# The key-length term of the attention heads, made by ScalarE with keys on partitions and turned into the score banks

## Chip, cores and metric

The kernel runs on one core of one Trainium2 chip. The metric is device microseconds from launch to end, the median of several runs. All data here is 32-bit float.

## What is computed

The kernel computes four small transformer layers one after another. The change touches only the attention of the last layer: 8 sequences of 512 tokens, 16 heads of 64 complex elements. Cut to what matters, for one head:

```python
qn = (q.real ** 2 + q.imag ** 2).sum(-1)          # length of each query
kn = (k.real ** 2 + k.imag ** 2).sum(-1)          # length of each key
E = exp(clip(-mu * |i - j|, -30, 0))              # depends on i - j alone
s = einsum('bihd,bjhd->bhij', qr, conj(kr)).real  # turned queries and keys
maha = maximum(qn[i] + E*E * kn[j] - 2 * E * s, 0) / V
logits = coef * log1p(maha / nu) - 0.5 * DH * log(V)
A = softmax(where(i >= j, logits, -inf));  out = A @ v
```

The kernel works with this expression divided by a function of i - j, so that a score is `s` plus a table times `kn[j]` plus another table times `qn[i]`. Every table depends on i - j alone. Before the heads start, each table lies in memory as one row per head, and is loaded so that partition p holds the row shifted by p. The lengths come out of the program with a factor of -0.5.

## The kernel before

The work of the heads is cut into 64 **pairs** m (a pair is two heads of one sequence: 8 sequences times 8 head pairs, 8 consecutive pairs sharing weights and tables) and each pair into two **units** g = 2m + e, one per head. A unit has four blocks i of 128 queries. Only the key blocks j <= i are worked on, ten blocks of 128 x 128, in three pieces p: `PIECES` (L3153) is block 3 (512 keys), blocks 1 and 0 (256 and 128 keys), block 2 (384 keys).

The order of the work is written out by hand. Each engine has a function (`heads_pe` L3173, `heads_dve` L3291, `heads_act` L3384, `heads_pool` L3492) with a loop `for m in range(-4, PAIRS + 1)` that issues its steps in one fixed order, for several pairs at once (a software pipeline). One pass through it is called a **turn** below. Each engine works through its list strictly in order and waits on counting semaphores (`k.after`). The SP queue issues the DMAs (`heads_loads` L2688).

A unit passes through these steps:

- TensorE `project` (L3176): queries (x = 0) and keys (x = 1) of a pair, two matrix products of 512 columns each, into banks 2 and 3. VectorE `products` (L3294) multiplies them by cosines and sines, GpSimd `rotate` (L3504, instructions L3511 and L3512) adds them, and the SP queue's `move` (L2677) copies the result by DMA to `qk`, of which there are two, for even and odd pairs.
- ScalarE `square` (L3387) squares `qk`. TensorE `norms` (L3188) sums over the elements into bank 1, ScalarE `lengths` (L3396) copies, TensorE `sums` (L3198) turns, and ScalarE `norms` (L3403) writes `nn`: the lengths with tokens on partitions. The squares of the keys are written in reverse order, so `nn` holds key lengths in reverse.
- GpSimd `norms` (L3495, instruction L3501) multiplies `backwards`, a matrix with ones on its anti-diagonal, by the key lengths: `dk`, four blocks of 128 x 128 for a unit.
- TensorE `scores` (L3206), one piece: for each query block a product of queries and keys into bank 4 + e, and for each of its key blocks a product of a table block with a block of `dk`, accumulated onto it.
- VectorE `query_norms` (L3309) adds the query term and moves the piece to `y`; `distance` (L3326); ScalarE `logarithm` (L3412); VectorE `logits` (L3337, a custom instruction with a minimum at L3346); ScalarE `exponential` (L3420).
- TensorE `flip` (L3226) turns each block, ScalarE `turned` (L3432) copies it to `pt`, TensorE `values` (L3252) multiplies by the values, which `project_values` (L3241) and ScalarE `values` (L3443) made. VectorE `reciprocals`, ScalarE `outputs` (L3451) and GpSimd `accumulate` (L3514, instruction L3524) close a unit.

Bank 4 + e holds one piece at a time: `scores` waits until `query_norms` has emptied it of the piece before. Products (`mm`, L74) show in the profile as line L75, transpositions (`tr`, L77) as L79. Both helpers issue one call, but the profile shows two MATMUL instructions with their weight loads for each 32-bit product and one for each transposition:

```python
def mm(self, out, lhsT, rhs, start=True, stop=True):
    return self.T.matmul(out, lhsT, rhs, start=start, stop=stop, skip_group_check=True)

def tr(self, out, in_, start=True):
    n = in_.shape[0]
    return self.T.matmul(out, in_, self.ident[0:n, 0:n], start=start, stop=True,
                         is_transpose=True, skip_group_check=True)
```

## Time and profile before

| | us |
|---|---|
| runs | 3070.5, 3072.42, 3085.04 |
| median | 3072.42 |
| the profiled execution | 3083.46, of which the span is 3082.2 |
| busy in the span: TensorE / VectorE / ScalarE / GpSimd | 2946.1 / 2434.7 / 1807.0 / 884.1 |
| mean granted clock of TensorE | 0.972 |

The span runs from the first to the last instruction of the profiled execution. Busy time is the time in which an engine has an instruction under way. Instructions of one engine overlap a little, so that the time to the next start is shorter than the duration shown. The heads start at about 1611 us and run to the end of the span; the rest is the earlier layers, which the change leaves alone.

### The profile page before, as it was taken

The numbers are of one execution on the slowest core, as the hardware profiler recorded it, in microseconds if no ns is written. First come the engines' busy times: TensorE is split into PE (matmuls) and PEld (weight loads), VectorE is DVE, ScalarE is ACT, GpSimd is POOL, SyncE is SP. The second block draws the span as 40 slices with busy tenths as digits, with TensorE's granted clock in tenths as the row PEclk, the third lists the DMA queues.
The fourth block names the chain that finished last, engine by engine and source line by source line (L and its number), as shares of the span: only waits on it lengthen the run. The fifth ranks groups of instructions, "written<-read, shape, count | busy, mean of one in ns | idle before, by whom it ended". The sixth has DMA issues, their size and how long they took to land. (4 is left out here: it accounts for less than half of the span.)

```text
span 3082.2 us, 55344 instructions
## 1 busy us (share of the span) xinstructions
PE 2946.1 (96%) x19062; PEld 2235.2 (73%) x19062; DVE 2434.7 (79%) x4760; ACT 1807.0 (59%) x4118; POOL 884.1 (29%) x839
## 2 busy tenths in 40 slices
PE   6999998999999999999687999999999999999998
PEld 4777775566666677787575787877878777878777
DVE  5878876566557555456766999999999999999997
ACT  3455544655645444434464777677777676776776
POOL 2111101101101100000433444444444444444442
PEclk8999999999999899999898999999999999999999
DMA  2000001000000000000402223232232323223221
GB/s 57 2 5 15 28 15 52 1 1 1 1 1 1 1 1 1 1 1 1 115 1 55 49 59 76 58 73 49 57 76 59 76 59 76 58 50 76 47 49 44
DMA packets 79513, 111.66 MB, mean 36 GB/s; under 512 B 15942, under 2 KB 32521, under 8 KB 79241
## 3 DMA queue, kind: packets, MB, share of 16 engines
q1 hardware_dynamic: 75266, 105.77, 14.3%
q8 instruction: 158, 2.59, 0.4%
q10 hardware_dynamic: 3974, 2.37, 0.3%
q14 instruction: 115, 0.93, 0.1%
HBM read 34.43 MB, written 6.55 MB: 13 GB/s over the span
## 5 line engine op out<-in xcount | busy, mean ns | idle before, releaser
L3346 DVE CUSTOM_DVE_ANT_0 scratch<-scratch,tb,coef 128x512 f32<-128x512 f32 (+3 forms) x512 | 552.9, 1115 | 1.3 <-ACT scratch L3418 1.3
L75 PE MATMUL banks<-lower 128*128 128x128 f32 (+2 forms) x2688 | 510.6, 356 | 1.4 <-DMA lower<-in_L_w2T 0.8
L75 PEld LDWEIGHTS banks<-lower 128*128 128x128 f32 (+1 forms) x2688 | 346.3, 195 | 166.4 <-issue 165.2
L75 PEld LDWEIGHTS banks<-scratch,tb 128*128 128x128 f32 x2560 | 357.3, 192 | 101.9 <-issue 61.9
L75 PE MATMUL banks<-scratch 128*128 128x256 f32 (+3 forms) x1088 | 378.1, 433 | 11.4 <-ACT scratch L3026 8.9
L3511 POOL TENSOR_TENSOR normed<-normed,aT 128x512 f32<-128x512 f32 x128 | 176.7, 1381 | 709.4 <-DVE aT L3304 426.0
L75 PE MATMUL banks<-scratch,tb 128*128 128x128 f32 x2560 | 369.4, 275 | 0.0
L75 PEld LDWEIGHTS banks<-n,pt 128*128 128x128 f32 x2560 | 300.8, 192 | 54.8 <-ACT pt L3440 51.1
L75 PE MATMUL banks<-n,pt 128*128 128x128 f32 x2560 | 323.5, 278 | 3.1 <-ACT moe L3459 3.1
L83 DVE SCALAR_TENSOR_TENSOR scratch<-scratch,tb 128x512 f32<-128x512 f32 (+3 forms) x512 | 320.8, 656 | 2.3
L83 DVE SCALAR_TENSOR_TENSOR scratch<-tb,nn,banks 128x512 f32<-128x512 f32 (+3 forms) x512 | 263.7, 535 | 41.1 <-PE banks L75 41.1
L3418 ACT ACTIVATE scratch<-scratch 128x384 f32<-128x384 f32 (+1 forms) x384 | 213.3, 556 | 137.6 <-DVE scratch L83 137.6
L3428 ACT ACTIVATE scratch<-scratch,mn 128x512 f32<-128x512 f32 (+3 forms) x512 | 288.0, 568 | 3.9 <-DVE mn L3346 3.9
L75 PE MATMUL banks<-nT,w 128*128 128x512 f32 x544 | 265.5, 610 | 10.5 <-DVE normed L3307 6.5
L1481 DVE TENSOR_TENSOR lower<-lower,banks 128x512 f32<-128x512 f32 x160 | 108.9, 685 | 157.7 <-ACT lower L1694 157.7
L3440 ACT ACTIVATE pt<-banks 128x384 f32<-128x384 f32 (+1 forms) x384 | 199.7, 528 | 48.9 <-PE banks L79 48.8
L79 PE MATMUL banks<-ident,scratch 128*128 128x128 f32 x1408 | 219.3, 273 | 3.0 <-ACT scratch L3428 2.1
L1694 ACT ACTIVATE lower<-banks 128x512 f32<-128x512 f32 x160 | 94.2, 597 | 199.2 <-PE banks L75 199.1
L75 PEld LDWEIGHTS banks<-scratch 128*128 128x128 f32 x1088 | 172.2, 192 | 47.1 <-issue 33.2
L3501 POOL TENSOR_TENSOR scratch<-backwards,nn 128x512 f32<-128x512 f32 x128 | 164.3, 1304 | 64.4 <-ACT nn L3410 64.4
L3459 ACT ACTIVATE moe<-banks,rs 128x128 f32<-128x128 f32 x512 | 145.6, 371 | 54.9 <-PE banks L75 54.9
L79 PEld LDWEIGHTS banks<-ident,scratch 128*128 128x128 f32 x1408 | 167.6, 142 | 8.3 <-issue 3.7
(433 smaller groups left out, 5448.3 us busy)
## 6 DMA issues: line engine op xcount, KB each, us to landing
scratch<-normed SPq DMA_DIRECT2D x512, 128.0 KB, 2.4
tb<-head_rows SPq DMA_DIRECT2D x32, 512.0 KB, 8.5
turn<-head_turns SPq DMA_DIRECT2D x32, 128.0 KB, 3.5
xs<-in_x SPq DMA_DIRECT2D x8, 256.0 KB
head_turns<-loads SPq DMA_DIRECT2D x8, 256.0 KB, 2.5
head_turns<-rotation SPq DMA_DIRECT2D x8, 256.0 KB, 2.8
w<-in_L_Wqk SPq DMA_DIRECT2D x8, 256.0 KB, 3.2
out<-xs SPq DMA_DIRECT2D x8, 256.0 KB, 2.3
```

Of the source, the lines that this page charges most:

```text
L75: return self.T.matmul(out, lhsT, rhs, start=start, stop=stop, skip_group_check=True)
L79: return self.T.matmul(out, in_, self.ident[0:n, 0:n], start=start, stop=True, is_transpose=True, skip_group_check=True)
L83: return self.V.scalar_tensor_tensor(out, a, s, b, op0, op1)
L1481: V.tensor_tensor(k.hidden[:, e % 2, m, b * S:(b + 1) * S], k.gated_h[:, m, :], k.bank(2 * m + 1), ALU.mult).then_inc(*k.l1_hid[m].up())
L1694: A.activation(k.gated_h[:, m, :], k.bank(2 * m), ACT.Silu).then_inc(*k.l1_silu[m].up())
L3346: x = V.tensor_tensor_reduce(y, y, view(hd["tb"][:, e, 2, i * P + 127:i * P + 128], [[-1, n]]), k.coef[:, h:h + 1], 3e38, ALU.add, ALU.min ...
L3418: A.activation(y, y, ACT.Ln, bias=1.0).then_inc(*k.h_ln.up())
L3428: x = A.activation(y, y, ACT.Exp, bias=t["mn"][:, i:i + 1], scale=-1.0, accum_out=t["sum"][:, i:i + 1])
L3440: A.activation(t["pt"][:, lo:hi], k.bank(6 + f % 2)[:, 0:hi - lo], ACT.Identity).then_inc(*k.h_pt.up())
L3459: x = A.activation(t["o"][:, i, :], k.bank(0)[:, i * P:(i + 1) * P], ACT.Identity, scale=t["rs"][:, i:i + 1])
L3501: G.tensor_tensor(t["dk"][:, :, :], k.backwards[:, :].unsqueeze(1).broadcast_to([P, 4, P]), r["nn"][:, :, 2 + e].unsqueeze(2).broadcast_to ...
L3511: G.tensor_tensor(re, re, k.sines[:, 1, :], ALU.subtract)
```

## The change

The key term of a unit is now made by ScalarE (`key_norms`): for each key block j, one activation reads the table of the key term with key p of the block on partition p and the queries from block j on along the row, and scales every partition by the length of its key. That gives `gk`, four tiles of 512, 384, 256 and 128 columns, of which there is one set per head e (before, `dk` had four). `scores` now first turns these blocks into the score bank with transpositions, and then accumulates the products of queries and keys onto them. The step of GpSimd goes away, and so do `backwards` and the reverse order of the squares. The table is loaded with another offset, by six DMAs of the same total size rather than four. The order of the steps in all four loops is new. Where the table's semaphore is waited for, 96 stands in place of 64.

```diff
@@ -2632,9 +2632,12 @@
         k.lengths = k.w1s.rearrange("p g h -> p (g h)")
         k.pairs3 = [dict(qk=flat[:, 2048 * j:2048 * j + 2048].rearrange("p (x e s) -> p x e s", x=2, e=2),
                          nn=k.sb(f"nn3_{j}", [P, TPB, 4])) for j in range(2)]
+        w2 = k.w2s.rearrange("p g d -> p (g d)")
+        gk = [[flat[:, a:b] for a, b in ((9216, 9728), (9728, 10112), (10112, 10368), (10368, 10496))],
+              [flat[:, 10496:11008], w2[:, 0:384], flat[:, 11008:11264], w2[:, 384:512]]]
         pt3 = [k.sb(f"pt3_{j}", [P, 1280]) for j in range(2)]
         k.lanes3 = [dict(y=flat[:, 4096 + 1280 * j:5376 + 1280 * j],
-                         dk=flat[:, 9216 + 512 * j:9728 + 512 * j].rearrange("p (t c) -> p t c", c=P),
+                         gk=gk[j % 2],
                          pt=pt3[j % 2], v=k.n[:, TPB * (j % 2):TPB * (j % 2) + TPB, :],
                          o=k.moe[:, TPB * (j % 2):TPB * (j % 2) + TPB, :],
                          mn=k.sb(f"mn3_{j}", [P, 4]), sum=k.sb(f"sum3_{j}", [P, 4]),
...
@@ -2670,9 +2673,9 @@
     def load_tables(self, hp):
         k, j = self, hp % 2
         for e in range(2):
-            for first in (0, 2):
-                k.Y.dma_start(k.head[j]["tb"][:, e, first:first + 2, :],
-                              k.spread(2 * hp + e, first, 2, 384)).then_inc(*k.h_tb[j].up(16))
+            for first, n, at in ((0, 2, 384), (2, 1, 384), (3, 1, 0)):
+                k.Y.dma_start(k.head[j]["tb"][:, e, first:first + n, :],
+                              k.spread(2 * hp + e, first, n, at)).then_inc(*k.h_tb[j].up(16))
 
     def move(self, m, x):
         k, Y = self, self.Y
...
@@ -3113,8 +3116,6 @@
-                k.fill(k.backwards[:, :], 0.0)
-                k.keep_where(k.backwards[:, :], ALU.not_equal, 1.0, 1 - P, [[1, P]], 1)
...
@@ -3210,17 +3211,18 @@
             k.after(T, k.h_mv, 128 * (m + 1))
             k.after(T, k.h_dk, g + 1)
             if m % SEQS == 0:
-                T.wait_ge(k.h_tb[m // SEQS % 2].sem, 64 * (m // SEQS // 2 + 1))
+                T.wait_ge(k.h_tb[m // SEQS % 2].sem, 96 * (m // SEQS // 2 + 1))
             k.after(T, k.h_qn, k.pieces(m, p, e) - 2)
-            at = 0
+            rows, at = [], 0
             for i in k.PIECES[p]:
-                n = (i + 1) * P
-                ps = k.bank(4 + e)[:, at:at + n]
-                k.mm(ps, r["qk"][:, 0, e, i * P:(i + 1) * P], r["qk"][:, 1, e, 0:n], stop=False)
+                rows.append((i, k.bank(4 + e)[:, at:at + (i + 1) * P]))
+                at += (i + 1) * P
+            for i, ps in rows:
                 for j in range(i + 1):
-                    x = k.mm(ps[:, j * P:(j + 1) * P], hd["tb"][:, e, 3, (i - j) * P:(i - j + 1) * P],
-                             t["dk"][:, 3 - j, :], start=False)
-                at += n
+                    k.tr(ps[:, j * P:(j + 1) * P], t["gk"][j][:, (i - j) * P:(i - j + 1) * P],
+                         start=(i == rows[0][0] and j == 0))
+            for i, ps in rows:
+                x = k.mm(ps, r["qk"][:, 0, e, i * P:(i + 1) * P], r["qk"][:, 1, e, 0:(i + 1) * P], start=False)
             x.then_inc(*k.h_sc.up())
 
         def flip(g, p):
...
@@ -3264,29 +3266,29 @@
 
         for m in range(-4, k.PAIRS + 1):
             values(2 * m - 1, 2)
-            flip(2 * m, 2)
+            scores(2 * m + 2, 2)
             scores(2 * m + 3, 2)
             sums(m + 2)
+            flip(2 * m, 2)
             project(m + 3, 1)
             project_values(2 * m + 1)
             flip(2 * m + 1, 0)
+            values(2 * m, 0)
+            flip(2 * m + 1, 1)
+            values(2 * m, 1)
+            flip(2 * m + 1, 2)
             scores(2 * m + 4, 0)
             scores(2 * m + 5, 0)
-            flip(2 * m + 1, 1)
-            values(2 * m, 0)
-            values(2 * m, 1)
+            scores(2 * m + 4, 1)
             values(2 * m, 2)
-            flip(2 * m + 1, 2)
             project(m + 4, 0)
-            scores(2 * m + 4, 1)
+            project_values(2 * m + 2)
             flip(2 * m + 2, 0)
             scores(2 * m + 5, 1)
-            project_values(2 * m + 2)
-            scores(2 * m + 4, 2)
             values(2 * m + 1, 0)
+            values(2 * m + 1, 1)
             flip(2 * m + 2, 1)
             norms(m + 3)
-            values(2 * m + 1, 1)
 
     def heads_dve(self):
         k, V = self, self.V
...
@@ -3313,7 +3315,7 @@
-                V.wait_ge(k.h_tb[m // SEQS % 2].sem, 64 * (m // SEQS // 2 + 1))
+                V.wait_ge(k.h_tb[m // SEQS % 2].sem, 96 * (m // SEQS // 2 + 1))
...
@@ -3356,30 +3358,30 @@
             V.reciprocal(t["rs"][:, :], t["sum"][:, :]).then_inc(*k.h_rs.up())
 
         for m in range(-4, k.PAIRS + 1):
-            query_norms(2 * m + 3, 1)
-            products(m + 3, 0, 1)
+            logits(2 * m + 1, 2)
             distance(2 * m + 3, 1)
-            reciprocals(2 * m)
             query_norms(2 * m + 2, 2)
-            distance(2 * m + 2, 2)
-            query_norms(2 * m + 3, 2)
             logits(2 * m + 2, 0)
             logits(2 * m + 3, 0)
+            query_norms(2 * m + 3, 2)
+            distance(2 * m + 2, 2)
             products(m + 3, 1, 1)
-            query_norms(2 * m + 4, 0)
             distance(2 * m + 3, 2)
             products(m + 3, 1, 0)
             logits(2 * m + 2, 1)
-            query_norms(2 * m + 5, 0)
+            query_norms(2 * m + 4, 0)
             logits(2 * m + 3, 1)
             logits(2 * m + 2, 2)
-            reciprocals(2 * m + 1)
+            query_norms(2 * m + 5, 0)
             distance(2 * m + 4, 0)
+            reciprocals(2 * m)
             query_norms(2 * m + 4, 1)
             distance(2 * m + 5, 0)
+            products(m + 4, 0, 0)
+            products(m + 4, 0, 1)
+            query_norms(2 * m + 5, 1)
+            reciprocals(2 * m + 1)
             distance(2 * m + 4, 1)
-            logits(2 * m + 3, 2)
-            products(m + 4, 0, 0)
 
     def heads_act(self):
         k, A = self, self.A
...
@@ -3390,8 +3392,7 @@
-            out = view(k.squares[1][:, 0, S - 1:S], [[S, 2], [-1, S]]) if x else k.squares[0]
-            A.activation(out, r["qk"][:, x, :, :], ACT.Square).then_inc(*(k.h_sk if x else k.h_sq).up())
+            A.activation(k.squares[x], r["qk"][:, x, :, :], ACT.Square).then_inc(*(k.h_sk if x else k.h_sq).up())
...
@@ -3408,6 +3409,20 @@
             k.after(A, k.h_dk, 2 * (m - 1))
             k.after(A, k.h_qn, 6 * (m - 1))
             A.activation(r["nn"][:, :, :], k.bank(1).rearrange("p (i c w) -> p i c w", i=TPB, c=4)[:, :, :, 0], ACT.Identity).then_inc(*k.h_nn.up())
+
+        def key_norms(g):
+            if not 0 <= g < k.UNITS:
+                return
+            m, e, t, r, hd = k.unit(g)
+            k.after(A, k.h_nn, m + 1)
+            if m:
+                k.after(A, k.h_sc, k.pieces(m - 1, 2, e))
+            if m % SEQS == 0:
+                A.wait_ge(k.h_tb[m // SEQS % 2].sem, 96 * (m // SEQS // 2 + 1))
+            for j in range(TPB):
+                x = A.activation(t["gk"][j], view(hd["tb"][:, e, 3, S - 1:S], [[-1, (TPB - j) * P]]),
+                                 ACT.Identity, scale=r["nn"][:, j, 2 + e:3 + e])
+            x.then_inc(*k.h_dk.up())
 
         def logarithm(g, p):
             if not 0 <= g < k.UNITS:
...
@@ -3462,44 +3477,37 @@
 
         k.nc.scalar.preload_act_table_set("natural_log_exp_and_others")
         for m in range(-4, k.PAIRS + 1):
+            exponential(2 * m + 1, 1)
+            logarithm(2 * m + 3, 0)
+            turned(2 * m, 0)
+            lengths(m + 2)
+            exponential(2 * m, 2)
+            logarithm(2 * m + 2, 1)
+            outputs(2 * m - 1)
+            norms(m + 2)
+            turned(2 * m, 1)
+            turned(2 * m, 2)
             exponential(2 * m + 1, 2)
+            key_norms(2 * m + 4)
+            turned(2 * m + 1, 0)
             logarithm(2 * m + 3, 1)
-            norms(m + 2)
             logarithm(2 * m + 2, 2)
-            turned(2 * m, 2)
+            key_norms(2 * m + 5)
+            exponential(2 * m + 2, 0)
+            turned(2 * m + 1, 1)
             values(2 * m + 1)
-            outputs(2 * m - 1)
-            exponential(2 * m + 2, 0)
-            turned(2 * m + 1, 0)
             exponential(2 * m + 3, 0)
-            turned(2 * m + 1, 1)
             square(m + 3, 0)
-            outputs(2 * m)
             logarithm(2 * m + 3, 2)
             turned(2 * m + 1, 2)
             exponential(2 * m + 2, 1)
             logarithm(2 * m + 4, 0)
-            exponential(2 * m + 3, 1)
+            outputs(2 * m)
             values(2 * m + 2)
             square(m + 3, 1)
-            logarithm(2 * m + 5, 0)
-            turned(2 * m + 2, 0)
-            turned(2 * m + 2, 1)
-            exponential(2 * m + 2, 2)
-            logarithm(2 * m + 4, 1)
-            lengths(m + 3)
 
     def heads_pool(self):
         k, G = self, self.G
-
-        def norms(g):
-            if not 0 <= g < k.UNITS:
-                return
-            m, e, t, r, hd = k.unit(g)
-            k.after(G, k.h_nn, m + 1)
-            k.after(G, k.h_sc, 6 * (m - 1))
-            G.tensor_tensor(t["dk"][:, :, :], k.backwards[:, :].unsqueeze(1).broadcast_to([P, 4, P]),
-                            r["nn"][:, :, 2 + e].unsqueeze(2).broadcast_to([P, 4, P]), ALU.mult).then_inc(*k.h_dk.up())
 
         def rotate(m, x):
             if not 0 <= m < k.PAIRS:
...
@@ -3525,12 +3533,10 @@
             x.then_inc(*k.h_acc.up())
 
         for m in range(-4, k.PAIRS + 1):
+            accumulate(2 * m - 2)
             rotate(m + 3, 0)
-            norms(2 * m + 4)
-            norms(2 * m + 5)
             rotate(m + 3, 1)
             accumulate(2 * m - 1)
-            accumulate(2 * m)
 
     def heads_close(self):
         k, V = self, self.V
```

## Rows read from the trace of the kernel before

**Rows 1.** Busy time by stretch: the stage before, the fill, a steady stretch.
```profile
...
core 0: us, PE busy (x) PEld busy (x) DVE busy (x) ACT busy (x) POOL busy (x), PEclk, DMA share, GB/s
1560.00:1600.00 40.00, 36.00 (x232) 30.42 (x232) 28.77 (x59) 32.36 (x73) 13.20 (x17) 1.00 0.00 1
1611.00:1640.00 29.00, 16.74 (x31) 6.10 (x32) 8.16 (x7) 4.32 (x6) 9.51 (x8) 0.65 0.24 55
...
2000.00:2300.00 300.00, 300.00 (x2054) 239.62 (x2053) 295.07 (x515) 212.28 (x569) 140.78 (x108) 1.00 0.28 65
...
```

**Rows 2.** The chain of waits, 2000 to 2100 us: start, us, what.
```profile
...
2002.49 4.43 PE banks L75 x34
...
2024.77 4.43 PE banks L75 x34
...
```

**Rows 3.** TensorE in order of time, part of one turn: start, us, what.
```profile
...
2016.49 1.02 PE L75 MATMUL banks<-scratch 128*128 128x512 f32 x2
2017.35 1.05 PE L75 MATMUL banks<-scratch,tb 128*128 128x128 f32 x8
2018.24 0.49 PE L79 MATMUL banks<-ident,scratch 128*128 128x128 f32 x3
2018.57 2.40 PE L75 MATMUL banks<-n,pt 128*128 128x128 f32 x20
...
2021.13 1.88 PE L75 MATMUL banks<-nT,w 128*128 128x512 f32 x4
2022.85 0.60 PE L75 MATMUL banks<-scratch 128*128 128x256 f32 x2
...
```

**Rows 4.** Groups by shape, 2000 to 2600 us: busy us, mean ns, idle before.
```profile
...
L75 PE MATMUL banks<-scratch,tb 128*128 128x128 f32 x1080 | 155.6, 275 | 0.0
...
L79 PE MATMUL banks<-ident,scratch 128*128 128x128 f32 x537 | 85.0, 273 | 0.0
...
L3459 ACT ACTIVATE moe<-banks,rs 128x128 f32<-128x128 f32 x212 | 60.3, 371 | 20.8 <-PE banks L75 20.8
...
L3418 ACT ACTIVATE scratch<-scratch 128x384 f32<-128x384 f32 x108 | 56.4, 522 | 10.7 <-DVE scratch L83 10.7
...
L3440 ACT ACTIVATE pt<-banks 128x384 f32<-128x384 f32 x108 | 53.2, 492 | 20.3 <-PE banks L79 20.3
L3428 ACT ACTIVATION_READ_ACCUMULATOR scratch<-scratch,mn 128x1 f32 x216 | 44.6, 207 | 0.0
...
L3418 ACT ACTIVATE scratch<-scratch 128x512 f32<-128x512 f32 x54 | 33.7, 624 | 50.6 <-DVE scratch L83 50.6
L3428 ACT ACTIVATE scratch<-scratch,mn 128x384 f32<-128x384 f32 x54 | 32.8, 607 | 0.0
...
```

**Rows 5.** ScalarE in order of time, two neighbours.
```profile
...
2005.29 1.05 ACT L3394 ACTIVATE hT<-scratch 128x1024 f32<-128x1024 f32 x1
2006.24 0.62 ACT L3418 ACTIVATE scratch<-scratch 128x512 f32<-128x512 f32 x1
...
```

**Rows 6.** GpSimd in order of time: key blocks, and both accumulations.
```profile
...
2012.16 2.50 POOL L3501 TENSOR_TENSOR scratch<-backwards,nn 128x512 f32<-128x512 f32 x2 [0.80 <-ACT nn L3410]
...
2021.82 2.73 POOL L3524 TENSOR_TENSOR acc<-acc,moe 128x512 f32<-128x512 f32 x2
...
```

**Rows 7.** VectorE in order of time, the same turn.
```profile
...
2005.08 0.61 DVE L3346 CUSTOM_DVE_ANT_0 scratch<-scratch,tb,coef 128x384 f32<-128x384 f32 x1
...
2010.24 0.58 DVE L83 SCALAR_TENSOR_TENSOR scratch<-tb,nn,banks 128x384 f32<-128x384 f32 x1
...
2012.23 1.52 DVE L3346 CUSTOM_DVE_ANT_0 scratch<-scratch,tb,coef 128x512 f32<-128x512 f32 x1
...
2015.13 1.21 DVE L3304 TENSOR_TENSOR aT<-banks,turn 128x1024 f32<-128x1024 f32 x1
...
```

**Rows 8.** The move's line on the DMA queue: ns min/median/max.
```profile
...
L2685 SPq DMA_DIRECT2D scratch<-normed x512: 461/597/2203, 1618.3 to 3026.3; - x171
...
```

**Rows 9.** The transpositions' line (L79) alone, by stretch.
```profile
...
1560.00:1600.00 40.00, 9.13 (x72) 8.39 (x73) 1.00 0.00 1
...
```

More of the change, by code:

```diff
@@ L2570, in layer3_prepare @@
         k.nT3, k.acc = k.sb("nT3", [D, SEQS, S]), k.sb("acc", [P, SEQS, TPB, D])
-        k.wvo, k.backwards = k.sb("wvo", [D, H, D]), k.sb("backwards", [P, P])
+        k.wvo = k.sb("wvo", [D, H, D])
         k.own, k.mu_scratch = k.sb("own", [P, 2, P]), k.sb("mu_scratch", [P, 2, 256])
```

## The prediction

> **What bounds the kernel now.** I read the busy time by stretch first. In a steady stretch of the heads TensorE is busy for all of 300 us at a granted clock of 1.00, VectorE for 295.07, ScalarE for 212.28, GpSimd for 140.78 [rows 1]. The chain of waits says what ends last: there TensorE's lines alone, the same piece returning after 22.28 us (2002.49, then 2024.77) [rows 2]. So a turn is 22.28 us and TensorE sets it: whatever leaves TensorE shortens the turn until another engine takes over. In the same units a turn has 21.91 us of VectorE (295.07 / 300 x 22.28), 15.77 of ScalarE and 10.46 of GpSimd. VectorE stands only 0.37 us below the bound, so its own gain decides how much of TensorE's can be had.
>
> **What leaves TensorE.** Ten key products a unit, 20 a turn, show as 40 MATMUL instructions a turn (1080 in 27 turns) [rows 4]. Eight follow each other in 0.89 us, from 2017.35 to the next start at 2018.24 [rows 3]: 0.111 each, 4.44 a turn. What comes in are 20 transpositions. They show as one instruction each (537 in 27 turns for the 20 flips), and the mean durations are alike, 275 and 273 ns [rows 4], so the spacing counts: three take 0.33 us (2018.24 to 2018.57) [rows 3], 0.110 each, 2.20 a turn. The products of queries and keys stay. **TensorE: 22.28 - 4.44 + 2.20 = 20.04 us a turn.** I take no price for changing between the two kinds, as three transpositions between products already come out at 0.33; that they now accumulate with products in one bank is not in the trace, and I bound it by 0 and 0.3 us a turn (twelve changes between the two kinds, a quarter of one instruction each).
>
> **What leaves VectorE.** No VectorE instruction goes; its saving is that GpSimd is not beside it. The two steps that go are 2.50 us of GpSimd from 2012.16 [rows 6], and VectorE's two instructions of 512 columns beside them take from 2012.23 to 2015.13, 2.90 us [rows 7] (two such, only the first is shown). One of 384 columns without GpSimd beside it takes 0.61, of which 0.54 until the next start. With 0.15 for 128 more columns that is 0.69, twice 1.38, so the pair lost 1.52 us. Instructions that read a bank lose nothing: 0.58 for 384 columns beside GpSimd at 2010.24 [rows 7]. With that pair gone and all else alike, **VectorE is 21.91 - 1.52 = 20.39 us a turn.** Six GpSimd instructions are left, 10.46 - 2.50 = 7.96 us. At the same price each (0.76) they cost 4.6 of the 20.39, so VectorE's own work is some 15.8. How much comes back depends on what the new order puts beside them. One accumulation now falls, after `outputs(2m)`, on the end of VectorE's list, where `products(m + 4, 0, ...)` read banks: up to 0.8 less. The other five fall on `distance` and `logits` as before. So 19.6 to 20.4.
>
> The Trainium skill, SBUF — State Buffer, "two separate sides", says that such a pair of ports is an exclusive lock and the loser fully blocks. By that, the two customs would have taken 2.50 + 1.38 = 3.88 us where the trace has 2.90, and taking GpSimd away would free 2.50, not 1.52: VectorE 19.4, TensorE alone the bound at 20.04. I go by the trace.
>
> **What ScalarE gets.** Eight activations a turn, per unit 512, 384, 256 and 128 columns. None is in the trace. The nearest are the logarithm (0.62 for 512 columns, 0.52 for 384) and `outputs` with the same kind of scale per partition (0.37 for 128) [rows 4]; for 256 between them, 0.45. Neighbours overlap by 0.10 (1.05 long, next start after 0.95) [rows 5]. That gives 0.52 + 0.42 + 0.35 + 0.27 = 1.56 a unit, 3.12 a turn, **ScalarE 15.77 + 3.12 = 18.9 us.** Bounds: 0.2 less a unit, and up to the price of the exponential instead (0.61 for 384), 0.1 more an activation, 19.7. Below 20.04 in every case, but with 1 us to spare, not 6.5.
>
> **Whether the waits close.** The key term was made by an engine with idle time; now it is queued on ScalarE, behind other steps and ahead of others. After `sums(m + 2)` TensorE has, until it needs `key_norms(2m + 5)` for `scores(2m + 5, 0)`: four flips of together 1.43, a projection of 1.72 (2021.13 to 2022.85), 0.89 for `project_values`, 0.89 and 0.67 for values, 1.30 for the piece of the other unit [rows 3]: 6.9 us. ScalarE has in that time `norms` 0.1, `turned` 0.38 twice, `exponential` 0.60 with the reading of its sum [rows 4], `key_norms` 1.56, `turned` 0.48, two logarithms of 0.41, `key_norms` 1.56: 5.9, and some 0.4 of waiting for `flip(2m + 1, 0)` between them, 6.3. It closes with 0.6 us. The other tight place is bank 4: `scores(2m + 4, 1)` comes right after `scores(2m + 5, 0)`, 1.30 us after the piece that `query_norms(2m + 4, 0)` must empty in 0.67; if VectorE is then inside an instruction that GpSimd holds up, TensorE waits a few tenths. I take **0.16 us a turn** for such places, 20.2, between 0 and what VectorE's unchanged losses give (20.4, and 0.2 more where it waits for TensorE).
>
> **Small ones.** The table's two extra DMA issues fall once in eight turns on the SP queue, at 0.6 us each as its move issues take [rows 8]; hidden by the queue's waits. The key lengths' order in the square costs nothing. The fill, where TensorE stands still more than a third of the time and the clock is at 0.65 [rows 1], gains nothing: 62 turns of 64 count.
>
> **The sum.** 62 x (22.28 - 20.2) = 129 us. The profiled execution took 3083.46, so it would be 2954. That execution lies 11 us above the median of 3072.42; nothing in the change touches where such executions differ, so I set the median at 3072.42 - 129 = **2943 us**.
>
> **Rivals.**
> - *VectorE takes over.* For it: 295.07 of 300 already. It decides if the new order gives back nothing: 20.4 plus waits of 0.3, 20.7, gives 98 us, 2974; if each of the 7.96 us held VectorE up in full, 15.8 + 8.0 = 23.8, past the old bound. Against that end: instructions on banks pass freely. Around 2974: 0.22.
> - *The key term arrives late (the slower end).* In place of the wait for GpSimd, `scores` waits for ScalarE's second `key_norms`. The slack is 0.6 us a turn, and each us beyond it costs 62 us. To lose against before, ScalarE must be 0.6 + 2.24 = 2.9 us later than worked out, which needs activations of about 0.75 rather than 0.39, or a `turned` or `exponential` ahead of them that itself waits for what TensorE does later, a loop. At 4 us late: 20.04 + 3.4 = 23.4, 3145. Against it: no activation of that size in the trace is so slow, and everything ahead in the list has its input from the turn before. 0.07, and 0.03 that it just eats the gain (within 0.5% of no change).
> - *The clock falls.* Transpositions double to 44 a turn, 2.2 per us. In the stage before there were 72 in 40 us, 1.8 per us [rows 9], with the clock at 1.00 and TensorE busy for 36 of 40 [rows 1]; in the fill, with TensorE idle, it went to 0.65. If it fell to the 1.2 GHz level for a tenth of the time, 20.04 / 0.95 = 21.1, 3000. 0.03. The Trainium skill, TensorE: Matmul & The Clock Gate, Part 4, says that transpositions do not count as activity for the gate; by that rule the doubled share speaks against this change, while the stretch just named, a fifth of it transpositions, kept the full clock.
> - *The change does more than I think:* TensorE alone binds, 20.04, 139 us, 2933. It is the lower part of my forecast, not a case apart.
>
> **How the numbers follow.** Forecast (20.04 to 20.4, 2933 to 2955) 0.65, VectorE 0.22, clock 0.03, slower 0.07, no change 0.03. About 0.5% (15 us) is what a measurement of this kernel can tell from no change. Faster by more: 0.90; I give 0.88, as part of VectorE's case reaches up to the old bound. Same 0.04, slower 0.08. The range: below, TensorE's 2933 less 10 for the differences between runs shown, 2923; above, VectorE's case to a turn of 21.1 (73 us), 3000.
>
> **What would show it.** Right: a turn has the 40 MATMUL of the key products no more, and 20 more under the transpositions' line; a turn of 20.0 to 20.4 in the chain, still TensorE's lines; VectorE at 20 us a turn or less and without the two stretched customs; ScalarE near 0.93. Wrong: a turn over 20.7; TensorE's weight loads of `gk` waiting on ScalarE's activation, or of `qk` on VectorE's `query_norms`; a granted clock under 1.00 after 1700 us; the stretched VectorE instructions costing more than 0.76 per GpSimd instruction.

## The result, and the profile after

The changed kernel takes 2947.01 us, the median of four runs (2941.78 to 2952.66), against 3075.39 us before; the ratio is 0.958, with a 95% interval of 0.955 to 0.961. The profiled execution took 2948.47 us. Forecast were 2943 and, for a profiled execution like the one before, 2954.

A **turn** is measured below from one start of TensorE's `norms` to the next. Before, 63 turns took 1399.97 us, nearly all of them 22.28. After, they take 1271.09 us: 128.9 us less. The profiled executions differ by 135.0. The other 6 us lie ahead of the first turn, which starts at 1631.80 before and 1625.14 after. In the profiles of this study that point falls anywhere from 1618.16 to 1637.46, so I count none of it as the change's. The tail behind the last turn is 50.4 us before and 50.6 after.

Busy time by stretch of the changed kernel, a row like that of [rows 1]:

```profile
...
core 0: us, PE busy (x) PEld busy (x) DVE busy (x) ACT busy (x) POOL busy (x), PEclk, DMA share, GB/s
2000.00:2300.00 300.00, 298.19 (x1963) 225.70 (x1961) 289.83 (x566) 282.17 (x745) 119.28 (x89) 1.00 0.31 73
...
```

TensorE is still the bound, but no longer for every nanosecond (298.19 of 300). VectorE is busy for nearly as large a share as before (289.83 against 295.07), in a shorter turn. ScalarE went from 212.28 to 282.17. The granted clock is 1.00.

The chain of waits of the changed kernel, to be held against [rows 2]: start, us, what.

```profile
...
by line: PE banks L75 69.3%; PE banks L79 21.6%; DMA scratch<-normed 3.6%; issue 2.2%; SPq L2688 1.7%; DVE scratch L3348 0.7%; DVE scratch L83 0.7%; DVE normed L3309 0.3%; DVE mn L3348 0.1%; SPq L3162 0.0%; DVEq L3162 0.0%
...
2003.56 2.22 PE banks L75 x18
...
2010.01 0.47 SPq L2688
...
2011.80 3.64 DMA scratch<-normed
2015.52 0.33 DVE normed L3309
...
2024.46 2.22 PE banks L75 x18
...
2044.51 2.22 PE banks L75 x18
...
```

From 2024.46 to 2044.51 is 20.05 us, and so are 22 of the 29 turns that lie between 2000 and 2600 us. From 2003.56 to 2024.46 is 20.90. In that turn the chain leaves TensorE: it goes over the SP queue and the queries' move to VectorE's product, which waits for the move to land.

The groups by shape of 2000 to 2600 us, with [rows 4] for before: of the 20 transpositions of key blocks in a turn 16 stand in the first group, with the 20 flips, and four in the group with the name w2s; the groups of L3423 are `key_norms`.

```profile
...
L79 PE MATMUL banks<-ident,scratch 128*128 128x128 f32 x1061 | 174.8, 274 | 4.8 <-DVE scratch L83 4.7
...
L3423 ACT ACTIVATE scratch<-tb,nn 128x512 f32<-128x512 f32 x59 | 42.3, 717 | 0.0
...
L79 PE MATMUL banks<-ident,w2s 128*128 128x128 f32 x118 | 30.6, 273 | 0.0
L3423 ACT ACTIVATE scratch<-tb,nn 128x256 f32<-128x256 f32 x58 | 29.0, 500 | 0.0
...
L3423 ACT ACTIVATE w2s<-tb,nn 128x384 f32<-128x384 f32 x29 | 17.5, 603 | 0.0
...
L3423 ACT ACTIVATE w2s<-tb,nn 128x128 f32<-128x128 f32 x29 | 11.3, 388 | 0.0
...
```

TensorE in order of time in the changed kernel, around the pieces of block 3 ([rows 3] before), and ScalarE's second `key_norms` of the same turn with the instruction behind it:

```profile
...
2036.35 0.93 PE L79 MATMUL banks<-ident,scratch 128*128 128x128 f32 x7
2037.12 1.02 PE L75 MATMUL banks<-scratch 128*128 128x512 f32 x2
2037.99 0.30 PE L79 MATMUL banks<-ident,scratch 128*128 128x128 f32 x1
2038.13 0.27 PE L79 MATMUL banks<-ident,w2s 128*128 128x128 f32 x1
...
2038.35 0.27 PE L79 MATMUL banks<-ident,w2s 128*128 128x128 f32 x1
2038.46 1.02 PE L75 MATMUL banks<-scratch 128*128 128x512 f32 x2
...
```

```profile
...
2035.98 0.71 ACT L3423 ACTIVATE scratch<-tb,nn 128x512 f32<-128x512 f32 x1
2036.60 0.60 ACT L3423 ACTIVATE w2s<-tb,nn 128x384 f32<-128x384 f32 x1
2037.11 0.49 ACT L3423 ACTIVATE scratch<-tb,nn 128x256 f32<-128x256 f32 x1
2037.51 0.39 ACT L3423 ACTIVATE w2s<-tb,nn 128x128 f32<-128x128 f32 x1
2037.80 0.71 ACT L3443 ACTIVATE scratch<-scratch,mn 128x512 f32<-128x512 f32 x1
...
```

Seven transpositions follow each other in 0.77 us (2036.35 to 2037.12), three flips and four key blocks: 0.110 each, with no price for changing between transpositions and products. Then comes the wait that mattered. The last activation of `key_norms` ends when the next starts to overlap it, about 2037.90, and the transpositions that need it start at 2037.99. The first stands 0.14 ahead of the second rather than 0.11. There is no slack at this place.

### The profile page after: what moved, and what is told of

It reads as the page before. It is cut to its first block and busy times, and to the rows that moved or that the text cites. A ratio compares the mean times of both kernels' runs of the same rounds, so it can differ in the third digit from the quotient of the medians.

```text
span 2946.8 us, 53185 instructions
## 1 busy us (share of the span) xinstructions
PE 2798.7 (95%) x17782; PEld 2064.2 (70%) x17782; DVE 2297.9 (78%) x4760; ACT 2018.7 (69%) x4630; POOL 725.8 (25%) x709
## 5 line engine op out<-in xcount | busy, mean ns | idle before, releaser
L79 PE MATMUL banks<-ident,scratch 128*128 128x128 f32 x2432 | 397.1, 274 | 17.2 <-DVE scratch L83 11.1
L3348 DVE CUSTOM_DVE_ANT_0 scratch<-scratch,tb,coef 128x512 f32<-128x512 f32 (+3 forms) x512 | 396.8, 810 | 0.8 <-ACT scratch L3433 0.8
L79 PEld LDWEIGHTS banks<-ident,scratch 128*128 128x128 f32 x2432 | 294.6, 142 | 114.8 <-issue 95.8
L75 PE MATMUL banks<-scratch 128*128 128x256 f32 (+3 forms) x1088 | 357.3, 433 | 8.9 <-ACT scratch L3029 8.9
L75 PE MATMUL banks<-n,pt 128*128 128x128 f32 x2560 | 344.5, 278 | 4.3 <-ACT moe L3474 4.2
L83 DVE SCALAR_TENSOR_TENSOR scratch<-scratch,tb 128x512 f32<-128x512 f32 (+3 forms) x512 | 343.8, 691 | 0.0
L3519 POOL TENSOR_TENSOR normed<-normed,aT 128x512 f32<-128x512 f32 x128 | 174.2, 1361 | 563.6 <-DVE normed L3309 481.6
L3532 POOL TENSOR_TENSOR acc<-acc,moe 128x512 f32<-128x512 f32 x120 | 164.9, 1374 | 236.3 <-ACT moe L3474 236.3
L3423 ACT ACTIVATE scratch<-tb,nn 128x512 f32<-128x512 f32 (+3 forms) x384 | 199.5, 574 | 0.1
L3309 DVE TENSOR_TENSOR normed<-banks,turn 128x1024 f32<-128x1024 f32 x128 | 156.1, 1220 | 46.0 <-DMA scratch<-normed 37.3
L3520 POOL TENSOR_TENSOR normed<-normed,aT 128x512 f32<-128x512 f32 x128 | 177.9, 1390 | 0.0
```

Of the source, the lines that this page charges most:

```text
L83: return self.V.scalar_tensor_tensor(out, a, s, b, op0, op1)
L3309: V.tensor_tensor(k.turned, k.bank(2, 2), cos_sin, ALU.mult).then_inc(*k.h_cos.up())
L3348: x = V.tensor_tensor_reduce(y, y, view(hd["tb"][:, e, 2, i * P + 127:i * P + 128], [[-1, n]]), k.coef[:, h:h + 1], 3e38, ALU.add, ALU.min ...
L3423: x = A.activation(t["gk"][j], view(hd["tb"][:, e, 3, S - 1:S], [[-1, (TPB - j) * P]]), ACT.Identity, scale=r["nn"][:, j, 2 + e:3 + e])
L3519: G.tensor_tensor(re, re, k.sines[:, 1, :], ALU.subtract)
L3520: G.tensor_tensor(im, im, k.sines[:, 0, :], ALU.add).then_inc(*k.h_rot.up())
```

## The experiments

The turns of all kernels in one table. "Commonest" is the length that occurs most often among the 48 turns from the tenth on (25 and 29 times in the two kernels without key transpositions, 27 times with the idle GpSimd pair, 36 times or more in the others), "mean" the mean over these turns, and the time is the median of the runs, or the only run. Kernels ran on different chips at different times, where the kernel before had medians from 3075 to 3081 us, so the turns compare better than the times.

| kernel | commonest | mean | time |
|---|---|---|---|
| before | 22.28 | 22.28 | 3075 |
| changed | 20.05 | 20.25 | 2947 |
| old term, new order | 22.28 | 22.29 | 3077 |
| new term, old order | 20.80 | 20.89 | 2988 |
| idle GpSimd pair | 20.52 | 20.77 | 2978 |
| no key transpositions | 19.43 | 19.87 | 2931 |
| tables spread | 20.05 | 20.12 | 2955 |
| tables spread, values later | 20.43 | 20.45 | 2965 |
| ScalarE idle step ahead | 20.46 | 20.54 | 2964 |
| ScalarE idle step behind | 20.05 | 20.21 | 2944 |
| key_norms early, values later | 19.98 | 20.04 | 2940 |
| key_norms early | 20.01 | 20.09 | 2948 |
| no key transpositions, key_norms early | 19.43 | 19.87 | 2926 |
| table slivers | 20.05 | 20.14 | 2947 |

**The order without the term.** The kernel before, with the four lists of the changed one; `key_norms` left out, GpSimd's `norms` kept behind `rotate(m + 3, 0)`:

```diff
             accumulate(2 * m - 2)
             rotate(m + 3, 0)
+            norms(2 * m + 4)
+            norms(2 * m + 5)
             rotate(m + 3, 1)
             accumulate(2 * m - 1)
```

> The kernel before with the changed kernel's order on all four engines (key term still by GpSimd and 32-bit products). My theory (the gain is TensorE's 2.24 us a turn, the order only makes room for it): TensorE keeps 22.28 us a turn, VectorE about 19.6 + 1.5 = 21.1, so the turn stays at 22.3 and the time within 10 us of before. Rival (the order is where the gain comes from): turn under 21.5, time under 3025 us. A third way, that the new order doesn't suit the old term: turn over 22.6.

Measured: ratio to before 0.999 (0.9975 to 1.0006), 22.28 us a turn. The order alone gains nothing in time; TensorE's 22.28 holds it. But VectorE says something that nobody expected. Busy time by stretch:

```profile
...
2000.00:2300.00 300.00, 300.00 (x2052) 239.19 (x2051) 266.85 (x513) 208.43 (x565) 138.91 (x108) 1.00 0.28 65
...
```

VectorE is busy for 266.85 us, where it was 295.07 [rows 1]: 19.8 us a turn rather than 21.9, with all eight GpSimd instructions in place. Its list holds the same instructions; they stand beside other company. GpSimd's key pair, and VectorE's instructions around it, in this kernel:

```profile
...
2013.97 2.37 POOL L3501 TENSOR_TENSOR scratch<-backwards,nn 128x512 f32<-128x512 f32 x2 [3.54 <-ACT nn L3410]
...
```

```profile
...
2012.48 0.75 DVE L3346 CUSTOM_DVE_ANT_0 scratch<-scratch,tb,coef 128x512 f32<-128x512 f32 x1
...
2013.16 0.75 DVE L3346 CUSTOM_DVE_ANT_0 scratch<-scratch,tb,coef 128x512 f32<-128x512 f32 x1
...
2013.83 0.61 DVE L83 SCALAR_TENSOR_TENSOR scratch<-tb,nn,banks 128x384 f32<-128x384 f32 x1
2014.36 1.07 DVE L83 SCALAR_TENSOR_TENSOR scratch<-scratch,tb 128x384 f32<-128x384 f32 x1
2015.75 1.23 DVE L3304 TENSOR_TENSOR aT<-banks,turn 128x1024 f32<-128x1024 f32 x1 [0.33 <-PE banks L75]
...
```

The custom instructions of 512 columns, which took 1.52 beside GpSimd [rows 7], take 0.75 here, since they are through before the pair starts. The pair now falls on `query_norms` and on `products`, which read banks, and on one `distance` (1.07 rather than 0.55).

**The term without the order.** The changed kernel with the lists of before:

```diff
             norms(m + 2)
+            key_norms(2 * m + 4)
             logarithm(2 * m + 2, 2)
             turned(2 * m, 2)
+            key_norms(2 * m + 5)
```

> The changed kernel with the orders of before on all four engines, the two key_norms put behind norms(m + 2) and behind turned(2m, 2). If the order hardly matters, TensorE's 20.04 to 20.3 us a turn stays and the time is within 10 us of 2947. My theory: the old order was laid out for a ScalarE with 6.5 us to spare a turn, and now waits appear; turn 20.8 to 21.6, time 2985 to 3035, about half of the gain. If the key term on ScalarE needs the new order altogether: turn 22 or more, 3060 or more.

Measured: 0.970 (0.968 to 0.972), 20.80 us a turn: seven tenths of the gain, more than the half I expected. VectorE is at 292.40 of 300, which is 20.4 us a turn, the 20.39 of the prediction. The rows of its waits, 2000 to 2600 us (total us, times, longest):

```profile
...
PEld banks L79 <- DMA scratch<-normed: 41.3, 34, 1.3
...
PE banks L79 <- DMA scratch<-normed: 15.5, 29, 0.5
DVE scratch L83 <- PE banks L75: 12.2, 29, 0.4
...
```

TensorE now waits in every turn for a move to land, ahead of the first transpositions of a piece, and stands idle for some 0.6 us a turn (it is busy for 291.33 of 300). That is the wait which the old order left no room for.

**GpSimd's company put back.** The changed kernel with two GpSimd instructions of 128 x 512 a turn that write a free buffer:

```diff
             rotate(m + 3, 0)
+            idle(2 * m + 4)
+            idle(2 * m + 5)
             rotate(m + 3, 1)
```

> The changed kernel with two GpSimd instructions of 128 x 512 a turn added where the key blocks used to be made; they write a buffer that nothing reads. If GpSimd's company was a price of its own (1.52 us of VectorE a turn in the kernel before): VectorE 20.5 to 21.2 us a turn rather than 19.6 and the turn 20.5 to 21.3, 15 to 65 us more. Rival (TensorE alone is the bound, VectorE has room): turn unchanged at 20.05 in most turns, mean 20.25, time within 6 us of the changed kernel.

Measured: 20.52 us in most turns, mean 20.77, 2978 us, 31 more. VectorE goes to 297.31 of 300, 20.6 us a turn, 1.1 more. TensorE alone is not the bound: with VectorE beyond 20.5, VectorE's list sets the turn.

**What stands behind TensorE.** No key transpositions; the key-length term is left out:

```diff
-            for i, ps in rows:
-                for j in range(i + 1):
-                    k.tr(ps[:, j * P:(j + 1) * P], t["gk"][j][:, (i - j) * P:(i - j + 1) * P],
-                         start=(i == rows[0][0] and j == 0))
             for i, ps in rows:
-                x = k.mm(ps, r["qk"][:, 0, e, i * P:(i + 1) * P], r["qk"][:, 1, e, 0:(i + 1) * P], start=False)
+                x = k.mm(ps, r["qk"][:, 0, e, i * P:(i + 1) * P], r["qk"][:, 1, e, 0:(i + 1) * P], start=(i == rows[0][0]))
```

> The changed kernel without the 20 key transpositions a turn: the key-length term is left out of the scores, ScalarE still makes its blocks. It asks what binds once TensorE has 2.20 us less, 17.85 a turn. My theory: VectorE with 19.6 and ScalarE with 19.1 us a turn stand right behind, so the turn goes only to 19.3 to 19.8, 28 to 55 us less. Rival (TensorE is the bound and nothing else is near): turn 17.9, 140 us less. Slow turns once in eight, which wait for a move, stay in either case.

Measured: 19.43 us in the commonest turn, mean 19.87, 2930.64 us, though TensorE's own work is 17.85. The commonest turn is in the range that I expected, the time is not: 16 us less rather than 28 to 55, since the turns behind the table loads are now much longer (23.0 to 23.2 in the worst of them). The next bound is 0.6 us below the present one, and an edit of this kind would be worth 0.4 us a turn on the mean, not 2.2. The bound is VectorE's own list: in turns of 19.43 it is never idle (19.43 us busy from 2002.04 to 2021.47), and nearly all its waiting between 2000 and 2600 us is for one thing, the landing of the queries' move (total us, times, longest):

```profile
...
DVE normed L3305 <- DMA scratch<-normed: 13.7, 17, 2.7
...
```

**Whether the second key_norms has slack.** One activation of 384 columns, put ahead of `key_norms(2m + 5)` in one kernel and behind `values(2m + 1)`, after both `key_norms`, in another:

```diff
             logarithm(2 * m + 2, 2)
+            idle(2 * m + 5)
             key_norms(2 * m + 5)
             exponential(2 * m + 2, 0)
             turned(2 * m + 1, 1)
             values(2 * m + 1)
+            idle(2 * m + 5)      (the other kernel)
```

> The changed kernel with one activation of 384 columns (about 0.4 us) added on ScalarE right ahead of key_norms(2m + 5). The prediction had 0.6 us between that step's end and scores(2m + 5, 0); the trace after shows the step ending at 2037.90 and the transpositions starting at 2037.99, next to nothing. If the chain from sums over both key_norms is tight: the turn grows by 0.3 to 0.4, to 20.4, 18 to 25 us more. Rival (ScalarE is busy for 19.06 of 20.05, so 0.4 fits in): turn 20.05 still, within 6 us.

> The same activation, behind values(2m + 1), that is after both key_norms. If only the chain up to key_norms(2m + 5) is tight: the turn stays at 20.05 to 20.1. If ScalarE's list as a whole is tight, wherever the work is put: 20.3 to 20.5, as with the activation ahead.

ScalarE in order of time, with the step ahead:

```profile
...
2036.96 0.51 ACT L3431 ACTIVATE mu_scratch<-nT 128x384 f32<-128x384 f32 x1
2037.37 0.72 ACT L3423 ACTIVATE scratch<-tb,nn 128x512 f32<-128x512 f32 x1
...
```

Measured: the step takes 0.41 us until the next start, and ahead of `key_norms` the turn grows from 20.05 to 20.46, by 0.41, all of it. Behind, it costs nothing: 20.05. ScalarE as a whole has room; the chain through `sums`, `norms` and both `key_norms` to `scores(2m + 5, 0)` has none. It was tight to within hundredths, as the rows of the changed kernel said.

**The long turns.** One or two turns in eight are longer in the changed kernel. The turns are counted from 0 below. First the table loads, one a turn instead of six in one turn:

```diff
...
-            if m % SEQS == 4 and 2 <= hp < k.HEADS // 2:
+            if m % SEQS >= 2 and 2 <= hp < k.HEADS // 2:
                 Y.wait_ge(k.h_sc.sem, 6 * done)
                 Y.wait_ge(k.h_lg.sem, 6 * done)
-                k.load_tables(hp)
+                k.load_tables(hp, m % SEQS - 2)
```

> The changed kernel with its six table loads of every eight turns issued one a turn, behind the keys' move, rather than all six in one turn. Its turns are 20.05 us but for two or three in eight of 20.4 to 21.6, mean 20.25. If the loads in flight hold up the queries' move of the next turn: the longer turn behind the load goes (index 12, 20, 28 ...), the mean falls to 20.12 to 20.18, 4 to 8 us less. If it is a single slow issue on the SP queue that has nothing to do with the loads (there is one of 1.85 us ahead of the load at 2011.80): the turns of index 11, 19, 27 ... stay at 20.9 and less than 4 us come back.

Measured: mean 20.12. The turns behind the loads (index 12, 28, 36, 44, 52) are 20.05 now, those of index 11, 19, 27 and so on stay at 20.3 to 21.0: about two thirds of the excess goes. (This run's 2955 us doesn't show it, since its first turn starts at 1637.46; its 63 turns take 1265.57 us, 5.5 less.) Then, in the changed kernel with its loads in one turn, the transfers cut from 128 partitions to one, so that the later heads' scores are made with wrong tables:

```diff
...
+                q = P if hp < 2 else 1
-                k.Y.dma_start(k.head[j]["tb"][:, e, first:first + n, :],
-                              k.spread(2 * hp + e, first, n, at)).then_inc(*k.h_tb[j].up(16))
+                k.Y.dma_start(k.head[j]["tb"][0:q, e, first:first + n, :],
+                              k.spread(2 * hp + e, first, n, at, q)).then_inc(*k.h_tb[j].up(16))
```

> The changed kernel with its table reloads cut from 128 partitions to one, so that later heads use the first tables (their scores are computed with wrong tables); number and place of the DMA issues are the same, the bytes are gone. If the transfers hold up the moves: all turns 20.05 but for the one slow issue in eight turns, mean 20.12 as with spread loads. If the slow single issue (1.85 us at 2011.80) also comes of the table loads: it goes too, mean 20.05. If the issues alone cost, not the bytes: mean 20.25 stays.

Measured: mean 20.14, the same picture. So the bytes in flight lengthen the turn behind them, and the other long turns (index 11, 19, 27 and so on) don't come of the table loads. In most of these an issue of the queries' move is slow. One in the changed kernel, and one in the kernel with slivers (0.60 is the common length):

```profile
...
2011.80 1.85 SPq L2688 DMA_DIRECT2D scratch<-normed  x1
...
```

```profile
...
2174.22 1.86 SPq L2689 DMA_DIRECT2D scratch<-normed  x1
...
```

But the slow issue alone doesn't explain them. In turns 11, 19 and 35 of the kernel with slivers no issue of this move takes over 0.60 us, and the last still lands 3.25 to 3.65 us after its start rather than the usual 2.4; the turns take 20.49 to 20.89. From the chain of waits in turn 11:

```profile
...
1851.94 0.60 SPq L2689
...
1852.58 3.26 DMA scratch<-normed
...
```

What these turns have in common is a packet on another DMA queue. The queues of the changed kernel from 2009.9 to 2016.5 us, around the slow issue at 2011.80 (packets, MB, share of 16 engines):

```profile
...
q1 hardware_dynamic: 320, 0.52, 34.8%
q8 instruction: 1, 0.02, 1.3%
...
```

The packet on q8, of a kind that the profile calls `instruction`, has 16 KB and lasts from 2011.85 to 2013.27. From turn 4 on, such a packet starts 5 to 7 us behind a turn's start, while the queries' move is under way, in turns 11, 19, 27, 35, 43, 51 and 59 and in no other, in the changed kernel and in the one with slivers alike. These are the long turns that are left (from turn 10 on, but for one of 20.26 with the spread loads). Of the changed kernel's move issues from turn 4 on, 24 of the 25 over 0.9 us overlap such a packet, and 41 of the 439 others. Between two packets lie on average 255.6 to 256.9 TensorE instructions (with those of its sequencer) in each of the fourteen profiles, whether 17.4 or 20.5 us pass between them, so they look like TensorE's own instructions being loaded. All this is read from the traces; no run moved these packets, and the cause is not shown by experiment. The kernel before has slow issues under such packets as well, 2.00 us at 1812.78 for one; nothing waited there.

**Values later.** Spread loads, and the moves started 0.67 us earlier:

```diff
-            values(2 * m - 1, 2)
             scores(2 * m + 2, 2)
             scores(2 * m + 3, 2)
+            values(2 * m - 1, 2)
             sums(m + 2)
```

> As the one before, and on TensorE values(2m - 1, 2) behind the two scores pieces, so that the queries' move starts 0.67 us earlier in a turn and a slow issue has that much more cover. My theory (TensorE binds at 20.05 and only late moves lengthen a turn): mean turn 20.05 to 20.12, 8 to 12 us less than the changed kernel, 2935 to 2939 against 2947. Rival (outputs(2m - 1) comes later by as much and ScalarE's chain is tight): every turn grows by up to 0.5 us, 2950 or more.

Measured: 20.43 us in nearly every turn, mean 20.45, ratio to before 0.963 (0.962 to 0.965). The rival was right. The long turns are nearly gone (20.5 to 20.7), but ScalarE's `outputs(2m - 1)` comes later, and with it `norms` and both `key_norms`. The chain of waits shows where:

```profile
...
2302.84 0.86 PE banks L75 x2
2303.70 0.28 issue
2303.98 0.63 PE banks L79 x4
...
```

TensorE stands still for 0.28 us ahead of the four transpositions of `scores(2m + 5, 0)`, and these take 0.63 rather than 0.44.

**Key_norms early.** If that is the chain, 0.82 us can be had by putting `key_norms(2m + 5)` ahead of two logarithms:

```diff
+            key_norms(2 * m + 5)
             logarithm(2 * m + 3, 1)
             logarithm(2 * m + 2, 2)
-            key_norms(2 * m + 5)
```

> The kernel with the spread table loads and values(2m - 1, 2) later, whose turns were 20.43 us, and in ScalarE's list key_norms(2m + 5) ahead of the two logarithms instead of behind them, 0.82 us earlier. If its 0.38 us a turn came from the chain outputs, norms, key_norms, scores: turns of 20.05 again, and as a late queries' move has 0.67 us more cover, 20.05 to 20.2 in the turns of index 11, 19 ... as well; mean 20.05 to 20.08, 2935 to 2942. Rival (the 0.38 us came over values(2m, 0) waiting for outputs(2m - 1), or the logarithms are now late for logits): turns stay at 20.3 to 20.5, 2955 or more.

> The same without the later values: the changed kernel with spread loads and the earlier key_norms. TensorE binds at 20.05, so the 0.82 us of slack gained buys nothing in most turns; the late queries' move stays (20.3 to 20.9 in one turn of eight). Mean 20.10 to 20.13, 2938 to 2945, 2 to 4 us more than the kernel with the later values. If the chain over key_norms was what made TensorE's 20.04 unreachable: 20.04 and nothing else changes.

> The kernel without the key transpositions (the key-length term is left out of the scores), whose turns were 19.43 us with TensorE at 17.85, with key_norms(2m + 5) ahead of the logarithms. If the 19.43 were set by the same chain over both key_norms: 18.9 to 19.2. If by VectorE's list (its waits and its instructions beside GpSimd): 19.4 as before, or up to 0.2 more for logarithms that come later.

Measured: with the later values 19.98 us in nearly every turn, mean 20.04, 2939.84 us (2934.86 to 2945.14), ratio 0.9551 (0.9529 to 0.9573); without them 20.01, mean 20.09, ratio 0.957 (0.955 to 0.959). The chain was the cause: the 0.38 us of the kernel with the later values go, and 0.07 more. Its 63 turns take 1261.16 us against 1271.09 of the changed kernel, 9.9 less. The ratios to before, 0.9551 and 0.9579, lean the same way, but their intervals overlap, so the better version is shown by its turns and not by its times. Without the later values the median is 2948.43 us, above the 2938 to 2945 expected and no less than the changed kernel's; its first turn starts 6.8 us later, and its 63 turns take 1264.52 us, 6.6 less. In the kernel without key transpositions the earlier `key_norms` changes nothing, 19.43 again, so this floor is not that chain's; VectorE's own list, which fills such a turn, sets it.

## Why the prediction was right

**The bound and TensorE's saving: right.** 40 MATMUL of 0.111 us out, 20 transpositions of 0.110 in, 20.04 us a turn worked out, 20.05 measured, 19.98 with a looser list. Accumulating products onto transpositions costs nothing.

**VectorE: the price was right in its place and wrong as a rule.** The step said that the pair of GpSimd instructions costs VectorE 1.52 us and that the others would fall on the same company as before. With the old order it is so: 21.91 to 20.4. With the new order VectorE stands at 19.5 us a turn, just under the 19.6 to 20.4 given, and the run with the old term shows why. There the order takes 2.1 us off VectorE (21.9 to 19.8), and taking the pair away afterwards only 0.3. The two savings are not a sum: by themselves they are 2.1 and 1.5, together 2.4. In the changed kernel the remaining instructions look as follows (GpSimd, then VectorE):

```profile
...
2024.71 1.29 POOL L3532 TENSOR_TENSOR acc<-acc,moe 128x512 f32<-128x512 f32 x1 [3.73 <-ACT moe L3474]
2026.66 1.29 POOL L3519 TENSOR_TENSOR normed<-normed,aT 128x512 f32<-128x512 f32 x1 [0.66 <-DVE aT L3306]
2027.90 1.45 POOL L3520 TENSOR_TENSOR normed<-normed,aT 128x512 f32<-128x512 f32 x1
...
```

```profile
...
2015.52 1.22 DVE L3309 TENSOR_TENSOR normed<-banks,turn 128x1024 f32<-128x1024 f32 x1 [1.40 <-DMA scratch<-normed]
...
2024.18 1.21 DVE L3309 TENSOR_TENSOR normed<-banks,turn 128x1024 f32<-128x1024 f32 x1
2025.31 1.21 DVE L3306 TENSOR_TENSOR aT<-banks,turn 128x1024 f32<-128x1024 f32 x1
...
2027.18 2.33 DVE L83 SCALAR_TENSOR_TENSOR scratch<-scratch,tb 128x256 f32<-128x256 f32 x2
...
2029.97 0.62 DVE L83 SCALAR_TENSOR_TENSOR scratch<-scratch,tb 128x256 f32<-128x256 f32 x2
...
2031.04 0.74 DVE L3348 CUSTOM_DVE_ANT_0 scratch<-scratch,tb,coef 128x512 f32<-128x512 f32 x1
...
2033.38 1.21 DVE L3306 TENSOR_TENSOR aT<-banks,turn 128x1024 f32<-128x1024 f32 x1
...
```

The accumulation at 2024.71 lies beside `products` that take their usual 1.21, as the step expected. Both instructions of one `rotate` lie on one `distance`, 2.33 us where its two parts take 0.62 alone (2029.97). The customs of 512 columns are alone, 0.74.

The Trainium skill, SBUF — State Buffer, "two separate sides", has the engine that starts first hold the ports for its whole instruction, while the other fully blocks. The case of `distance` fits it better than the pair before did: it runs from 2027.18 to the next start at 2029.43, and GpSimd ends at 2029.35. The custom pair of [rows 7] remains shorter than that rule gives.

**ScalarE: the total was right, the single price too low.** 18.9 us a turn were forecast, 19.0 measured. But four activations take 1.82 us (2035.98 to 2037.80) rather than 1.56. The logarithm and the bare copy were the wrong neighbours; the exponential, my upper end, was the right one (0.71 for 512 columns in the trace after). The total came out by luck: the 0.52 us that two `key_norms` take more are partly made up by the order, which alone brings ScalarE from 15.77 us a turn to 15.5 (208.43 of 300, in the run with the old term).

**The slack: wrong.** "It closes with 0.6 us" is the step that failed. Two `key_norms` at 0.26 more each take 0.52 of the 0.6, and the activation put ahead shows that nothing was left. The rows of the changed kernel agree: from the end of `sums` (2031.09) TensorE took 6.90 us to the transpositions at 2037.99, as worked out, and ScalarE 6.81 rather than 6.3. The number came out unharmed by luck: TensorE's own 20.04 and the chain's end meet at the same place, and 0.4 us more on ScalarE would have made 20.46 of it. Of the rival in which the key term arrives late, the place and the price were right (0.41 us more on ScalarE, 0.41 us more a turn), the distance to it was not.

**The 0.16 us a turn: near in size by luck (0.20 measured), wrong in cause.** I gave it to the chain and to bank 4. TensorE waits at neither in most turns. The mean of 20.25 comes from one to two turns in eight that wait for the queries' move. "Hidden by the queue's waits" was my step for the SP queue. It looked at the queue's idle time, not at who waits for the landing: with VectorE's list shortened, `products(m + 3, 1, 0)` stands right behind it (1.40 us of idle at 2015.52 in the rows above, where a turn of 20.05 has 0.4 or less). The two issues more are not what costs: with their bytes gone and the issues in place, the turns behind the loads are 20.05.

**The clock: right.** With 44 transpositions a turn it stays at 1.00. The Trainium skill, TensorE: Matmul & The Clock Gate, Part 4, says that transpositions don't count as activity for it; here, where they are a quarter of TensorE's time and never more than seven in a row, that rule had no effect that a row shows.

## What to carry to other kernels

A product with a matrix that only permutes is a transposition in disguise: let the engine with time to spare do the scaling, and TensorE the turning, at one instruction instead of two for 32-bit data. When work moves to an engine that others wait for, work out the chain it now stands in with the dearest price of its kind, since the total of that engine says nothing about slack. And what GpSimd costs VectorE is a property of the order: put it beside instructions that read a bank before taking work away from it.

## What the runs showed of the hardware

- Eight GpSimd instructions of 128 x 512 a turn cost VectorE 2.1 us a turn more or less, by their neighbours alone (295.07 against 266.85 us busy of 300).
- A move's DMA issue on the SP queue that takes 0.60 us takes 0.9 to 2.2 now and then, in all fourteen kernels, with the table transfers or without. 261 of these 263 issues (from turn 4 on) overlap a 16 KB packet of queue q8, of which one comes for every 256 TensorE instructions. Under one, the last two DMAs of a move land after 3.8 and 3.6 us rather than 2.4 (issues at 2011.15 and 2011.80).
- An activation of a table in SBUF with a scale per partition takes 0.72 us for 512 columns and 0.60 for 384, as dear as an exponential (0.71 and 0.61), not as a copy out of a bank (0.60 for 512).
